# Router on groups of four tiles, and expert counts scanned on VectorE ahead of the rank matmuls

## The chip, the cores and the metric

The kernel runs on one NeuronCore of a Trainium2 chip. The metric is device time in microseconds, the median of three runs. The engines are called PE (TensorE, matmuls), PEld (its weight loads), DVE (VectorE), ACT (ScalarE), POOL (GpSimd) and SP (SyncE, which here only issues DMAs). "q" behind an engine's name is its instruction queue.

## The reference

32 sequences of 64 rows of 512 numbers are first mixed by a 64x64 matrix that is looked up per sequence, then go through a router and a mixture of eight experts (each token takes its two best, an expert takes at most 640), and the result is added to the input.

```python
def cond(x, conditions, weights):
    w = weights[conditions]
    return jnp.einsum('bct,bcd->bdt', x, w)

def ffn(x, Wr, Wg, Wu, Wd):
    N = Bb * Tt
    cap = max(1, int(1.25 * (N * 2 / E)))
    xf = x.reshape(N, Hh)
    logits = jnp.einsum('nh,eh->ne', xf, Wr)
    gate = jax.nn.softmax(logits, axis=-1)
    top2_val, top2_idx = jax.lax.top_k(gate, 2)
    flat_idx = jnp.concatenate([top2_idx[:, 0], top2_idx[:, 1]])
    onehot = jax.nn.one_hot(flat_idx, E, dtype=jnp.int32)
    rank = (jnp.cumsum(onehot, axis=0) * onehot).sum(-1)
    keep = rank <= cap
    ...
    g = jax.nn.silu(jnp.einsum('nh,eih->eni', xf, Wg))
    u = jnp.einsum('nh,eih->eni', xf, Wu)
    out_e = jnp.einsum('eni,ehi->enh', g * u, Wd)
    y = jnp.einsum('ne,enh->nh', comb, out_e)

x = x + ffn(cond(x, itok_B_1_198, cond_weights), Wr, Wg, Wu, Wd)
```

## The kernel before

The 2048 tokens lie in 16 tiles of 128 rows, in pairs m = 0 to 7 (tile j belongs to pair j // 2). The program has two parts. The front finds out which token goes to which expert and writes the conditioned tokens to the DRAM buffer `xf_dram`. The expert part gathers rows of `xf_dram` expert by expert and runs the three projections in split fp32r. All engines have hand-written instruction streams with semaphores; what stands in the source is the order in which each engine works, and an engine stops at each wait.

The front has two strands that meet at the first gather.

The **routing strand**. `x_tile_turn(j)` transposes a tile of x on PE (L1178, four 128x128 transposes into one PSUM bank), ACT (L601) or DVE (L811, tiles 1, 2, 5, 6 and 9) copies it to `turned_sb`. `router(m)` multiplies one pair by the router weights: four matmuls of 256 columns, one for each quarter of the 512 features, each in its own group of 32 PE columns (L1190). DVE copies the result (`xrT_copy`, L818), PE turns it back (`turn`, L1201), DVE adds the four quarters (`xr_sum`, L824), and `logits(g)` multiplies by the conditioning matrices (L1223), in four groups of tiles given by `LG` (6, 4, 4 and 2 tiles). `top_two` finds the two best experts of each token (MAX and MAX_INDEX, one of each for each tile, L832 and L835), and `one_hot` (L845) writes them as ones into `ohp` for tiles 0 to 7 and 8 to 15. After the second one_hot PE sums the counts of each tile over all 128 rows (L1269) and within the tile (L1272); DVE scans the totals (L902), adds the rank within the tile (L905), multiplies by the one-hot (L906) and reduces to one rank for each assignment (L907). From this come slot numbers, the comparison tables `pick_t` and `pick_p` (L924, L927, L930), 32 small PE matmuls that invert the list (L1283) and `src_row` (L951), which releases `lists_ok`.

The **conditioning strand**. `condition(j)` multiplies one pair of x tiles by its matrices on PE (eight matmul records of 512 columns, L1234) into two of four PSUM banks; it waits until ACT has copied the pair before the previous one out of its banks. ACT copies each tile to `xf_sb` (L593), SP stores each pair to `xf_dram` (L390, the last two tiles apart on L394). `condition(0)` to `condition(6)` stand ahead of the rank matmuls on PE, `condition(8)` to `condition(14)` behind them. ACT also makes the rounded high parts of the first expert's weights, `w_high(u)` (L609), one of four between these copies (`W0_EARLY = 1`), three behind them, and DVE the low parts, `w0_low(u)` (L942).

POOL waits for `lists_ok` and for every store (`xf_out`) before its first gather (L508). PE fills the time until that has landed with matmuls whose result is not used (`KEEP_WARM = 18`, L1289), then turns the gathered rows (L1303) and starts the first expert.

SP loads x in eight DMAs of two tiles, then two small ones, places eight tiles' conditioning matrices (L361), loads the first expert's gate and up weights (L372), stores `xf_dram`, then the gates (L396, waits for `gates_ok`), and then loads the first expert's down weights (L376, L379).

## Time and profile before

| | us |
|---|---|
| median of three runs | 274.7 (273.92 to 275.18) |
| the profiled execution | 272.44 |
| its span, first to last instruction | 270.6 |
| PE busy | 257.8 (95% of the span) |
| first gather issued by POOL | 37.55 |
| first gathered rows turned by PE | 42.09 |

The span is read by stretches: up to 42 us the front, then eight experts in which PE is the engine with the most work. An instruction's start and duration in the timeline are read as they stand; what ended the idle time ahead of it stands in brackets behind it.

### The profile page before, as it was taken

To read this page: it belongs to the slowest core of one execution; us is meant where nothing else is said; L and a number is where in the kernel's file an instruction comes from. 1 tells how busy PE (TensorE), PEld (TensorE's weight loads), DVE (VectorE), ACT (ScalarE), POOL (GpSimd) and SP (SyncE) were. 2 spreads that over 40 slices of the span, in tenths; PEclk is the share of its full clock that TensorE was granted. 3 is DMA by queue.
4 is the path that set the end of the run, shared out by engine and by line. 5 is a ranking of instruction groups with operands and counts; after the bars stand their busy time and mean duration, and the time that the engine had idled before them with its cause. 6 is when DMAs were issued, how large, how long until landed. Compare 5 with 4: busy or idle time off the path is not lost.

```text
span 270.6 us, 4016 instructions
## 1 busy us (share of the span) xinstructions
PE 257.8 (95%) x1368; PEld 200.0 (74%) x1368; DVE 161.6 (60%) x332; ACT 137.7 (51%) x242; POOL 173.6 (64%) x156
## 2 busy tenths in 40 slices
PE   8999698999999999999999999999999999999991
PEld 4663156999987867888878887777787777878980
DVE  2658998444459664876566639674865867343251
ACT  2356843444464656565366644664565559442100
POOL 5792048741158867884887478858887886685742
PEclk9999979999999999999999999999999999999998
DMA  6996888999869998899679867998899699366441
GB/s 201 363 300 241 344 270 272 386 338 330 294 193 209 202 207 256 162 216 277 170 130 250 238 178 111 200 294 251 154 238 329 148 192 225 40 79 81 131 177 46
DMA packets 27099, 59.00 MB, mean 218 GB/s; under 512 B 6198, under 2 KB 6454, under 8 KB 26976
## 3 DMA queue, kind: packets, MB, share of 16 engines
q1 hardware_dynamic: 16416, 37.89, 44.3%
q0 software_dynamic: 10656, 20.75, 37.2%
q8 instruction: 16, 0.26, 0.4%
q14 instruction: 11, 0.09, 0.1%
HBM read 39.56 MB, written 20.25 MB: 221 GB/s over the span
## 4 chain that ended last, share of the span: by engine, by line
PE 52%; DVE 3%; ACT 2%; DMA 2%; issue 2%; POOLq 0%; ACTq 0%; DVEq 0%
PE bank L1342 19%; PE bank L1429 17%; PE bank L1437 9%; PE bank L1316 3%; DMA xg<-xf_dram,src_turn 2%; PE bank L1444 2%; PE bank L1452 2%; DVE w L1005 1%; ACT hhi L696 1%; POOLq L85 0%; DVE squares L1054 0%; PE bank L1303 0%; DVE hlo L1060 0%; DVE h L1120 0%; DVE h_last L1100 0%
## 5 line engine op out<-in xcount | busy, mean ns | idle before, releaser
L1429 PE MATMUL bank<-xhi,w 128*128 128x512 f32 x280 | 71.6, 398 | 0.0
L1342 PE MATMUL bank<-w,hhi 128*128 128x512 f32 (+1 forms) x216 | 67.1, 393 | 1.5 <-ACT y_sb L667 1.0
L554 POOL DMA_INDIRECT out<-y_sb,dst_row x35 | 56.5, 1613 | 13.4 <-issue 13.4
L1429 PEld LDWEIGHTS bank<-xhi,w 128*128 128x128 f32 x280 | 52.3, 188 | 13.2 <-DVE h_last L1100 0.8
L520 POOL DMA_INDIRECT gate_g<-gates_dram,src_row x40 | 46.8, 1170 | 12.1 <-issue 11.5
L1342 PEld LDWEIGHTS bank<-w,hhi 128*128 128x128 f32 x216 | 39.2, 188 | 10.7 <-DVE hlo L1060 1.6
L1005 DVE TENSOR_TENSOR w<-raw,w 128x704 fp32r<-128x704 f32 (+1 forms) x35 | 37.1, 1060 | 14.6 <-ACT w L609 8.2
L508 POOL DMA_INDIRECT xg<-xf_dram,src_turn x24 | 25.6, 1065 | 26.0 <-DVE xlo L990 11.6
L1342 PE MATMUL bank<-w,hlo 128*128 128x512 f32 (+1 forms) x108 | 41.9, 388 | 0.0
L1437 PE MATMUL bank<-xlo,w 128*128 128x512 f32 x140 | 38.4, 396 | 0.0
L609 ACT ACTIVATE w<-raw 128x704 fp32r<-128x704 f32 (+1 forms) x40 | 36.7, 923 | 0.0
L508 POOL DMA_INDIRECT xg<-xf_dram,src_row x16 | 18.1, 1130 | 27.5 <-DMA xf_dram<-xf_sb 15.9
L1054 DVE STREAM_TRANSPOSE squares<-xg 128x512 f32<-128x512 f32 x24 | 24.0, 1046 | 16.7 <-DMA xg<-xf_dram,src_turn 16.7
L1437 PEld LDWEIGHTS bank<-xlo,w 128*128 128x128 f32 x140 | 26.4, 189 | 6.4
L667 ACT ACTIVATE y_sb<-bank,gate_g 128x512 f32<-128x512 f32 x30 | 20.1, 686 | 20.0 <-PE bank L1342 18.6
L1342 PEld LDWEIGHTS bank<-w,hlo 128*128 128x128 f32 x108 | 20.3, 188 | 4.6
L1316 PE MATMUL bank<-w,xhi 128*128 128x352 f32 x112 | 20.5, 327 | 0.8 <-ACT xhi L644 0.8
L1316 PEld LDWEIGHTS bank<-w,xhi 128*128 128x128 f32 x112 | 18.2, 189 | 1.4 <-issue 1.0
L696 ACT ACTIVATE hhi<-h 128x512 fp32r<-128x512 f32 x14 | 8.9, 634 | 19.6 <-DVE h L1107 12.0
L1060 DVE TENSOR_TENSOR hlo<-h,hhi 128x512 fp32r<-128x512 f32 x14 | 9.7, 693 | 10.4 <-ACT hhi L696 10.4
L990 DVE TENSOR_TENSOR xlo<-xg,xhi 128x512 fp32r<-128x512 f32 x24 | 15.0, 684 | 1.5 <-ACT xhi L654 1.5
L654 ACT ACTIVATE xhi<-xg 128x512 fp32r<-128x512 f32 x24 | 13.3, 620 | 2.7 <-DMA xg<-squares 2.7
(138 smaller groups left out, 304.8 us busy)
## 6 DMA issues: line engine op xcount, KB each, us to landing
raw<-wgu SPq DMA_DIRECT2D x32, 352.0 KB, 7.8
xg<-squares SPq DMA_DIRECT2D x24, 256.0 KB, 7.5
x_sb<-x SPq DMA_DIRECT2D x8, 512.0 KB, 7.6
raw<-wd SPq DMA_DIRECT2D x8, 512.0 KB
xf_dram<-xf_sb SPq DMA_DIRECT2D x7, 512.0 KB, 3.0
raw<-wd SPq DMA_DIRECT2D x8, 192.0 KB
out<-x SPq DMA_DIRECT2D x1, 1280.0 KB, 18.3
gate_g<-gates_dram,src_row POOLq DMA_INDIRECT x40, 6.5
```

Source lines behind the costliest of these rows:

```text
L508: nc.gpsimd.indirect_dma_start(out=xg[:, t, :], out_offset=None, in_=xf_dram[:, :], in_offset=bass.IndirectOffsetOnAxis(ap=rows, axis=0), ...
L520: nc.gpsimd.indirect_dma_start(out=gate_g[:, n % TPE, :], out_offset=None, in_=gates_dram[:, :], in_offset=bass.IndirectOffsetOnAxis(ap=sr ...
L554: nc.gpsimd.indirect_dma_start(out=out[:, :], in_=y_sb[:, n % TPE, :], in_offset=None, out_offset=bass.IndirectOffsetOnAxis(ap=dst_row[:, ...
L609: last = nc.scalar.activation(w[:, half, 0, a:b], raw[:, a:b], ACT.Copy)
L667: nc.scalar.activation(y_sb[:, t, :], y_bank(e, t)[:, :], ACT.Copy, scale=gate_g[:, t, e:e + 1]).then_inc(y_ok, n)
L990: nc.vector.tensor_tensor(xlo4[:, :, cols], turned_rows(e, t), xhi4[:, :, cols].bitcast(F32), ALU.subtract).then_inc(xlo_ok, n)
L1005: last = nc.vector.tensor_tensor(w[:, half, 1, a:b], raw[:, a:b], w[:, half, 0, a:b].bitcast(F32), ALU.subtract)
L1054: nc.vector.transpose(squares[:, :, t, :], xg[:, t, :].rearrange("p (i b) -> p b i", i=SQ)).then_inc(squares_ok, 1)
L1316: last = nc.tensor.matmul(ps[:, 0:I], left[:, b, c], w[:, half, part, o:o + I], start=(k == 0 and left is xhi and part == 0), stop=(k == K ...
L1342: last = nc.tensor.matmul(ps[:, cols], left(c), w[:, half, part, o:o + width], start=(c == 0 and q == 0), stop=(closes and c == cs[-1] and ...
L1429: last = nc.tensor.matmul(ACC_BANK[what][:, :], columns(what, k, part), xhi4[:, k, :], start=(k == 0 and part == 0), stop=False)
L1437: last = nc.tensor.matmul(ACC_BANK[what][:, :], columns(what, k, 0), xlo4[:, k, :], start=False, stop=(k == KH - 1))
```

## The change

- The router takes four tiles at a time: four matmuls of 512 columns instead of two sets of four with 256. Tiles 0 to 11 keep their turned copy in a buffer of their own (`turned_x`, over memory that is used only later), so the copies no longer wait for the router. `turn`, `xrT_copy` and `xr_sum` also take four tiles; two of the four `xrT` copies are on ACT.
- The last two tiles come from DRAM already turned (a new input `xt`, 512 KB, prepared with the other inputs), and PE doesn't turn them. Their router step is in two halves of 256 columns for each quarter. The natural-order tiles 14 and 15 (`load_x(7)`) are loaded behind the placed matrices.
- `LG` is four groups of four tiles. `top_two` of the last two groups is one block of DVE instructions.
- `condition(0)`, `(2)` and `(4)` stand ahead of the rank matmuls, `condition(6)` to `(14)` behind them; before, `(6)` was ahead too.
- The counts are scanned over tiles and experts on DVE first (`before`, a bf16 tile), and PE multiplies the scan by ones and adds it in PSUM onto the ranks within the tile. DVE then needs one multiply and one reduce.
- Softmax: one subtract for tiles 0 to 11 and one for 12 to 15, one exponential of all tiles on ACT behind its fourteenth `xf_copy`, the sums behind `pick_p`, the gate product behind the lists.
- All four `w_high` of the first expert are behind the sixteen `xf_copy`, all four `w0_low` behind the lists. The first expert waits for two of them ahead of its first half and for four ahead of the second.
- `KEEP_WARM` is 27 instead of 18.

```diff
-LG = ((0, 3), (3, 5), (5, 7), (7, NM))
+LG = ((0, 2), (2, 4), (4, 6), (6, NM))
+RING = 3 * XR
+TURNED = TT - 2
-KEEP_WARM = 18
+KEEP_WARM = 27
...
-            for m in range(2, NM):
+            for m in range(2, NM - 1):
                 load_x(m)
+            sp.dma_start(turned_x[:, RING:RING + 2, :, :],
+                         xt.rearrange("p (r k c) -> p r k c", r=2, k=KH)).then_inc(xt_in, 16)
...
             for j in range(HALF, TT):
                 place(j)
+            load_x(NM - 1)
...
-            sp.wait_ge(gates_ok, 2)
+            sp.wait_ge(gates_ok, 1)
...
+            for g in range(XRT_DVE, NG):
+                act.wait_ge(xrT_ps, g + 1)
+                nc.scalar.activation(xrT[:, g % 2, :], ps_xrT[g][:, :],
+                                     ACT.Copy).then_inc(xrT_ok, 1)
...
+            for n in range(TT):
+                xf_copy(n, n % XR)
+                if n == TT - 3:
+                    act.wait_ge(sub_ok, 2)
+                    nc.scalar.activation(ex[:, :, :], lg[:, :, :], ACT.Exp).then_inc(ex_ok, 1)
+            for u in range(KH):
                 w_high(u, 0, 0)
...
             dve.wait_ge(oh_ok, 2)
+            dve.wait_ge(oh_clear, 1)
+            dve.wait_ge(consts, CONSTS)
+            nc.vector.tensor_tensor_scan(before[:, :, :].rearrange("p e a -> p (e a)"),
+                                         carry[:, :, :].rearrange("p e a -> p (e a)"),
+                                         ohp[:, :, :].rearrange("p e a -> p (e a)"), 0.0,
+                                         ALU.mult, ALU.add).then_inc(before_ok, 1)
+            subtract(0, LG[3][0] * 2)
             dve.wait_ge(rank_ps, 1)
...
-            link(nc.vector.tensor_tensor(rk[:, :, :], run[:, :, 0:A], within, ALU.add))
-            link(nc.vector.tensor_tensor(rk[:, :, :], rk[:, :, :], oh, ALU.mult))
+            ranks = ps_rank.rearrange("p (e a) -> p e a", e=E)
+            nc.vector.tensor_tensor(rk[:, :, :], ranks[:, :, 0:A], oh,
+                                    ALU.mult).then_inc(before_ok, 1)
...
-            for u in range(W0_EARLY):
-                w0_low(u)
...
+            gate_sums()
             dve.wait_ge(slot_ps, 1)
...
+            gates()
+            for u in range(KH):
                 w0_low(u)
...
+            turn_tiles(0, 8)
+            pe.wait_ge(wr_in, 16)
+            router(0)
+            turn_tiles(8, 12)
+            router(1)
+            turn(0)
+            turn_tiles(12, TURNED)
+            turn(1)
+            logits(0)
+            router(2)
+            logits(1)
+            router(3)
             condition(0)
-            router(NM - 1)
-            turn(NM - 2)
-            condition(2)
-            turn(NM - 1)
+            turn(2)
+            turn(3)
             logits(2)
             logits(3)
+            condition(2)
+            condition(4)
...
-            nc.tensor.matmul(ps_total, ones[:, :], o, start=True, stop=True)
...
+                nc.tensor.matmul(ranks[:, :, o_j:A:2], left[:, :], oh[:, :, o_j::2],
+                                 start=(o_j == 0), stop=False)
+            pe.wait_ge(before_ok, 1)
+            for cols in (slice(0, A), slice(A, A + 1)):
+                last = nc.tensor.matmul(ranks[:, :, cols], ones[:, :], before[:, :, cols],
+                                        start=False, stop=(cols.start == A))
             last.then_inc(rank_ps, 1)
-            for j in range(after, TT, 2):
+            for j in range(6, TT, 2):
                 condition(j)
...
                 if s == 0:
-                    pe.wait_ge(wlo0_ok, KH)
+                    pe.wait_ge(wlo0_ok, 2)
...
+                if s == 0:
+                    pe.wait_ge(wlo0_ok, KH)
```

PE's queue around the ranks, before (L1234 is a pair of `condition`, L1269 and L1272 are the rank matmuls, L1283 the list matmuls):

```order
L1234 MATMUL bank<-x_sb,wq 64x512 [waits xf_ok]
L1234 MATMUL bank<-x_sb,wq 64x512 x3
L1269 MATMUL bank_7<-ohp,ones 128x264 [waits oh_clear,oh_ok,consts]
L1272 MATMUL bank_7<-ohp,upper 128x128
L1272 MATMUL bank_7<-ohp,upper_odd 128x128
L1234 MATMUL bank<-x_sb,wq 64x512 [waits xf_ok]
L1234 MATMUL bank<-x_sb,wq 64x512 x3
```

And in the changed program, from the second to the fourth pair (`condition` is L1235, the rank matmuls are L1274 and L1278):

```order
L1235 MATMUL bank<-x_sb,wq 64x512 [waits x_in1]
L1235 MATMUL bank<-x_sb,wq 64x512 x3
L1235 MATMUL bank<-x_sb,wq 64x512 [waits xf_ok,x_in2]
L1235 MATMUL bank<-x_sb,wq 64x512 x3
L1274 MATMUL bank_7<-ohp,upper 128x8x16 [waits oh_clear,oh_ok,consts]
L1274 MATMUL bank_7<-ohp,upper_odd 128x8x16
L1278 MATMUL bank_7<-before,ones 128x8x32 [waits before_ok]
L1278 MATMUL bank_7<-before,ones 128x8
L1235 MATMUL bank<-x_sb,wq 64x512 [waits xf_ok,x_in3]
L1235 MATMUL bank<-x_sb,wq 64x512 x3
```

The pair that waits for `x_in3` (tiles 6 and 7) has moved behind the ranks, and a second wait, for `before_ok`, now stands ahead of it and of all later pairs.

ACT's queue from the last copy of a turned tile, before (L593 is `xf_copy`, L620 the exponential, L609 `w_high`; behind the branch a loop of two rounds with four copies each, of which the first is shown):

```order
L593 ACTIVATE xf_sb<-bank 128x512 [waits xf_ps] x2
L620 ACTIVATE ex<-lg 128x80 [waits sub_ok]
L593 ACTIVATE xf_sb<-bank 128x512 [waits xf_ps] x2
L609 ACTIVATE w<-raw 128x704 [waits raw_in0]
L593 ACTIVATE xf_sb<-bank 128x512 [waits xf_ps] x2
L620 ACTIVATE ex<-lg 128x48 [waits sub_ok]
L593 ACTIVATE xf_sb<-bank 128x512 [waits xf_ps] x2
L634 UNCONDITIONAL_BRANCH
L634 ISA
L593 ISA [waits xf_ps]
L593 ACTIVATE xf_sb<-bank 128x512
```

And in the changed program (L618 is the copy of `xrT`, L605 `xf_copy`, L636 the exponential, L625 `w_high`):

```order
L618 ACTIVATE xrT<-bank_7 128x512 [waits xrT_ps]
L618 ACTIVATE xrT<-bank 128x512 [waits xrT_ps]
L605 ACTIVATE xf_sb<-bank 128x512 [waits xf_ps] x14
L636 ACTIVATE ex<-lg 128x128 [waits sub_ok]
L605 ACTIVATE xf_sb<-bank 128x512 [waits xf_ps] x2
L625 ACTIVATE w<-raw 128x704 [waits raw_in0]
```

Nothing but one exponential stands between the copies now; the weights' high parts are all behind them.

## Rows read from the trace of the kernel before

**Rows 1.** The profile's page, its first lines: span, and PE's busy time.

```profile
span 270.6 us, 4016 instructions
PE 257.8 (95%) x1368; PEld 200.0 (74%) x1368; DVE 161.6 (60%) x332; ACT 137.7 (51%) x242; POOL 173.6 (64%) x156
```

**Rows 2.** Timeline, SP and POOL at the front's end: start, duration, engine, line, instruction.

```profile
35.05 0.65 SPq L376 DMA_DIRECT2D raw<-wd  x1
...
37.55 1.73 POOL L508 DMA_INDIRECT xg<-xf_dram,src_row  x1 [15.88 <-DMA xf_dram<-xf_sb]
```

**Rows 3.** Line L486, POOL's wait for the stores (duration ns, first and last start us).

```profile
L486 POOLq EVENT_SEMAPHORE  x1: 17/17/17, 36.8 to 36.8; - x1
```

**Rows 4.** DMA issues: the last store of xf, and the first gather (us to landing).

```profile
xf_dram<-xf_sb SPq DMA_DIRECT2D x1, 256.0 KB, 3.3
xg<-xf_dram,src_row POOLq DMA_INDIRECT x1, 4.4
```

**Rows 5.** Timeline, ACT's copies of the conditioned tiles, and three w_high behind them.

```profile
27.16 1.09 ACT L593 ACTIVATE xf_sb<-bank 128x512 f32<-128x512 f32 x2
29.02 2.06 ACT L593 ACTIVATE xf_sb<-bank 128x512 f32 x4 [0.76 <-PE bank L1234]
31.40 2.06 ACT L593 ACTIVATE xf_sb<-bank 128x512 f32 x4 [0.32 <-PE bank L1234]
33.35 2.16 ACT L609 ACTIVATE w<-raw 128x704 fp32r<-128x704 f32 x3
```

**Rows 6.** Timeline, PE from the ranks to the first expert.

```profile
27.76 1.95 PE L1234 MATMUL bank<-x_sb,wq 64*64 64x512 f32 x16
33.72 2.53 PE L1283 MATMUL bank<-pick_t,turned_sb 128*128 128x40 f16 x32 [1.50 <-DVE turned_sb L930]
36.08 5.75 PE L1289 MATMUL bank<-iota_q 128*128 128x512 f16 x18
42.09 0.63 PE L1303 MATMUL bank<-ident,xg 128*128 128x128 f32 x4 [0.26 <-DMA xg<-xf_dram,src_row]
```

**Rows 7.** Timeline, PE in the router's stretch, and one burst of weight loads.

```profile
10.92 1.09 PE L1178 MATMUL bank<-ident,x_sb 128*128 128x128 f32 x8
13.75 0.64 PE L1190 MATMUL bank<-turned_sb,wr_sb 128*32 128x256 f32 x8
14.32 0.44 PE L1201 MATMUL bank<-ident,xrT 128*128 128x128 f32 x2
14.59 1.04 PE L1178 MATMUL bank<-ident,x_sb 128*128 128x128 f32 x8
20.73 0.41 PE L1223 MATMUL bank<-xr,wq 64*64 64x8 f32 x16
25.36 0.18 PEld L1234 LDWEIGHTS bank<-x_sb,wq 64*64 64x64 f32 x4 [0.25 <-ACT xf_sb L593]
```

**Rows 8.** Timeline, DVE from a top_two to the rank chain and the tables.

```profile
21.21 0.39 DVE L832 MAX8 v<-bank 128x8 f32<-128x8 f32 x4
22.34 0.24 DVE L864 TENSOR_TENSOR lg<-bank,v 128x80 f32<-128x80 f32 x1
26.86 0.38 DVE L845 TENSOR_TENSOR ohp<-iota_e,i 128x128 bf16<-128x128 f32 x1
27.92 0.70 DVE L902 TENSOR_TENSOR_SCAN run<-carry,bank 128x264 f32<-128x264 f32 x1
29.57 0.59 DVE L907 TENSOR_REDUCE r<-rk 128x32 f32<-128x256 f32 x1
32.89 2.49 DVE L930 TENSOR_TENSOR turned_sb<-iota_q,slot_tp 128x1024 f16<-128x1024 f16 x4
36.29 0.20 DVE L951 TENSOR_SCALAR src_row<-bank 128x40 uint32<-128x40 f32 x1
```

**Rows 9.** Stretches of 0.5 us: PE, PEld, DVE, ACT, POOL busy, then PE's granted clock.

```profile
37.50:38.00 0.50, 0.50 (x3) 0.20 (x2) 0.50 (x2) 0.00 (x0) 0.45 (x1) 0.50 0.93 328
40.50:41.00 0.50, 0.50 (x4) 0.20 (x2) 0.47 (x2) 0.00 (x0) 0.32 (x1) 1.00 0.71 283
```

More of the change, by code:

```diff
@@ L127, in build @@
         oh = ohp[:, :, 1:A + 1]
-        run = sb("run", [P, E, A + 1])
+        before = sb("before", [P, E, A + 1], BF16)
         more = sb("more", [1, E], U16)
@@ L204, in build @@
         wsel_in = sem("wsel_in")
-        row_in = [sem(f"row_in{g}") for g in range(len(LG) - 1)]
-        placed = [sem(f"placed{g}") for g in range(1, len(LG))]
+        row_in = [sem(f"row_in{g}") for g in range(2)]
+        placed = [sem(f"placed{g}") for g in range(2, NG)]
+        xt_in = sem("xt_in")
         tT_ps = sem("tT_ps")
@@ L279, in build, with turned_slot @@
         TURN_DVE = [1, 2, 5, 6, 9]
-        TURN_ACT = [j for j in range(TT) if j not in TURN_DVE]
+        TURN_ACT = [j for j in range(TURNED) if j not in TURN_DVE]
+        def turned_slot(j):
+            return j % RING if j < TURNED else RING + j - TURNED
         def group_of(j):
@@ L849, in one_hot @@
                     ALU.is_equal).then_inc(oh_ok, 1)
[L851 to L860 removed]
+            for j in TURN_DVE[0:4]:
+                turn_copy(j)
+            xrT_copy(0)
+            for j in TURN_DVE[4:]:
+                turn_copy(j)
+            xrT_copy(1)
+            xr_sum(0)
+            xr_sum(1)
+            top_two(0)
+            top_two(1)
+            xr_sum(2)
             def subtract(a, b):
@@ L933, in _ @@
                     ALU.is_equal).then_inc(pick_ok, 1)
-            nc.vector.tensor_scalar(more[:, :].unsqueeze(2), run[0:1, :, A:A + 1],
-                                    -float((TPE - 1) * P), 0.0,
-                                    ALU.add, ALU.max).then_inc(more_ok, 1)
             def w0_low(u):
@@ L967, in _ @@
                                     ALU.add).then_inc(lists_ok, 1)
-            for u in range(W0_EARLY, KH):
+            gates()
+            for u in range(KH):
                 w0_low(u)
@@ L1180, in x_tile_turn, with router @@
                 last.then_inc(tT_ps, 1)
-            def router(m):
-                for j in (m * 2, m * 2 + 1):
+            def router(g):
+                for j in range(g * XR, min((g + 1) * XR, TURNED)):
                     turned(j)
-                if m >= 1:
-                    pe.wait_ge(xrT_ok, m)
-                r = m * 2 % XR
+                if g == NG - 1:
+                    pe.wait_ge(xt_in, 16)
+                if 1 <= g < NG - 1:
+                    pe.wait_ge(xrT_ok, g)
@@ L1203, in turn @@
+                last.then_inc(xrT_ps, 1)
+            def turn(g):
+                pe.wait_ge(xrT_ok, g + 1)
+                if 1 <= g < NG - 1:
+                    pe.wait_ge(xr_ok, g)
+                for j in range(XR):
+                    last = nc.tensor.transpose(ps_xr[g][:, j * P:(j + 1) * P],
+                                               xrT[:, g % 2, j * P:(j + 1) * P], ident[:, :])
                 last.then_inc(xr_ps, 1)
@@ L1216, in logits @@
                 if by_place:
-                    pe.wait_ge(placed[g - 1], 16 * len(by_place))
+                    pe.wait_ge(placed[g - 2], 16 * len(by_place))
                 if 0 < g < 3:
```

173 lines of the change are left out of this document (62 added, 111 removed).

## The prediction

> **What bounds the kernel now.** I read three views in this order. The page gives the span and PE's share: 95% of 270.6 us [rows 1]. From 42 us on PE has little idle time, so a change of the front is worth what it moves the moment at which PE turns the first gathered rows, 42.09 us [rows 6], nearly one for one. The timeline's end of the front then tells what sets that moment. Two strands meet at the first gather. The lists: `src_row` is written at 36.29 and done at 36.49 [rows 8]. The stores of xf: ACT's last copy ends at 31.40 + 2.06 = 33.46 [rows 5], the last store lands 3.3 us behind its issue [rows 4], and POOL's wait ends at 36.8 [rows 3]. So the stores come last, by 0.3 us; the two strands are nearly level. The gather starts at 37.55 [rows 2] and lands 4.4 us later [rows 4], PE turns at 42.09. From the end of the last copy to that turn it is 42.09 - 33.46 = 8.63 us.
>
> The third view is ACT's and PE's rows of the conditioning strand. Copies run in groups of four tiles of 2.06 us with gaps of 0.76 and 0.32 us that PE ends [rows 5]. Four tiles and a gap are 2.38 us: two PSUM pairs turn over between an engine that needs 0.98 us for a pair (1.95 for two [rows 6]) and one that needs 1.03. What sets the last copy is therefore the moment at which PE resumes conditioning behind the ranks, 27.76 us [rows 6], and how many pairs are left then: four.
>
> **The router's stretch, step by step.** x arrives as before up to tile 7; PE turned tiles 6 and 7 at 10.92 [rows 7] as they landed, and that stays, since the DMAs ahead of them are the same. What changes is that the gaps ahead of it held routers before and stay empty now. So I start the new PE sequence at 10.92 and add it up:
> - turning tiles 6 to 13, four pairs: a pair occupies PE for 0.98 us until the router's start at the pace of [rows 7]; 3.9;
> - four routers: four matmuls of 512 columns in four column groups are not in the trace. A set of 256 columns holds PE 0.57 us (13.75 to 14.32 [rows 7]); four matmuls of 512 columns in four quadrants hold it 0.98 us [rows 6]. The bounds are 0.57 and 1.14 (two sets); I take 0.98, the row with the same number of columns; 3.9;
> - four turns of four tiles: two take 0.27 until the next instruction (14.32 to 14.59 [rows 7]); 0.5 each; 2.0;
> - logits of four tiles 0.3 to 0.4 each (0.41 for sixteen records [rows 7]); 1.3; `condition(0)` 0.98;
> - new waits: `logits(1)` waits for the first `top_two`, 1.13 us long for four tiles (21.21 to 22.34 [rows 8]), which `router(2)` covers but for 0.4; `logits(2)` and `(3)` wait for two reduces, 0.7.
>
> Together 13.2 us: `logits(3)` ends near 24.1. Then `top_two` of eight tiles: one of four takes 1.13, the MAX part of the first four overlaps the last logits, so 1.9 to its end; subtract and one_hot 0.5. The second one_hot ends at about T = 26.45, against 26.86 + 0.38 = 27.24 [rows 8]. The routing strand gains 0.8 us up to here. `condition(2)` and `(4)` lie in PE's wait, and cost nothing as long as they end by T: 24.1 + 2 x 0.98 = 26.1, just so.
>
> **The ranks.** Before, PE's rank matmuls needed only the one_hot, and `condition(8)` stood 0.52 us behind T (27.76 - 27.24). Now the DVE scan stands between: 0.70 us [rows 8] and a semaphore to each side. PE can resume at T + 0.05 + 0.70 + 0.3 = T + 1.05 = 27.5; the 0.3 for the semaphore and the ones matmul is an estimate from the 0.52, which held the same steps and three matmuls. What is queued behind that wait on PE is all remaining conditioning, five pairs now. For DVE the chain is shorter: before, the reduce (L907) ended at 29.57 + 0.59 = T + 2.92 [rows 8], after two gate steps and the add; now scan, the ones matmul, multiply and reduce give T + 2.35. The tables follow as before (5.2 us to the end of `pick_p`, 35.38, [rows 8]): `pick_p` ends at 26.45 + 2.35 + 5.2 = 34.0.
>
> **The conditioning strand, which decides.** The first pair behind the ranks leaves PE 0.98 later, and ACT starts its copy at 27.5 + 1.26 = 28.8 (before, 27.76 to 29.02 [rows 5, 6]). Five pairs are two groups of four tiles and one pair: 28.8 + 2.06 + 0.32 + 2.06 + 0.32 + 1.03 = 34.6. The one exponential fits into the second gap (its wait for the subtracts is long over). Removing `w_high` (0.8 us) between the early copies gives nothing: these copies now end long before PE resumes. So the last copy ends at 34.6 instead of 33.46: **+1.1 us**. The moment of resuming gained 0.26 us, the fifth pair costs 1.35.
>
> **Behind it.** PE ends conditioning near 33.4, when three of four `pick_p` are written, and needs about 2.4 us for the 32 list matmuls (2.53 [rows 6]): 35.8. The lists are then ready at 36.1, some 0.4 earlier than before, which buys nothing, since the stores land at 36.8 + 1.1 = 37.9. The gather starts at 38.65 and lands at 43.1. The warm matmuls: 18 took 5.75 us [rows 6], with the granted clock at 0.50 (1.2 GHz) in a part of it and 1.00 (2.4 GHz) again by 40.5 [rows 9]. About 3.4 us at the lower clock and 2.35 at the higher make 0.225 us for one at full clock, and nine more 2.0 us. From 35.8 they end at 35.8 + 5.75 + 2.0 = 43.6, half a us behind the landing, and the turn waits for that: 43.7. If the clock doesn't fall they end at 41.9 and the landing sets 43.2. So the turn is 1.1 to 1.6 us later. A third piece pulls the same way: the gates' product stands behind the lists now, so SP stores the gates and loads the first down weights (704 KB, issued at 35.05 before [rows 2]) some 3 us later, right into the gather's transfer; zero to 0.5 us, and partly under the warm matmuls' overrun. I take +1.5 for the sum.
>
> What has cover: the four `w_high` (2.16 for three [rows 5]) end at 37.5 and the four `w0_low` near 41, before PE's first use near 44.4. The copies of `src_turn` stand behind them and are the thinnest cover: they end about when ACT has the first rounded rows, and would cost if the lists came later. The 512 KB of `xt` are in the place of x's last pair; that pair, behind the placed matrices, is needed only at 32 us. The relaxed wait for the first expert's weights releases nothing that is late.
>
> **Sum.** 272.44 + 1.5 = 273.9 in a profiled execution like the one shown, whose span is 270.6; on the median of the three runs 274.7 + 1.5 = **276.2 us**. The measurement can tell about 0.5%, 1.4 us, from no change; the forecast lies on that edge.
>
> **Rivals.**
> (1) *The last router is slow.* It puts two matmuls on one column group and then goes on to the next. If the next group can't start before the second half has, it holds PE for 3 x 0.49 + 0.98 = 2.45 us instead of 0.98. T, PE's resuming and all that follows are 1.5 us later: 277.7. Against it: in two successive pairs of `condition`, the weights of four quadrants are loaded in one burst at 25.36 [rows 7], while earlier passes still ran in each, so a waiting quadrant didn't hold up the others. A depth of more than two waiting passes isn't in the trace, so half of the price is possible too. The Trainium skill, TensorE: Matmul & The Clock Gate, Part 3 (The mechanism), says that matmuls start and end strictly in program order and only weight loads are pulled ahead; by that rule this rival is the outcome. The same price would arise if PE's granted clock fell from 1.00 to 0.50 in the stretches that are empty now, ahead of 10.92 and around 27 us. Chance 0.2.
> (2) *The front is level or gains.* If a router of 512 columns cost 0.6 us like one of 256, T would be 25.0 and PE would resume at 26.1; the last copy ends at 33.2, and the stores at 36.5. The point from which this decides is a resuming at 26.4 us or earlier. Then the turn is at 41.8 and the time 274.4; and if ACT's gaps of 0.76 and 0.32 are its loop's branches, which the change unrolls, rather than PE's lag, up to 1.0 more goes: 273.4. For it: the row of 256 is not at its columns' rate alone. Against it: the condition rows, which are. Chance 0.2 with gains of under 1.4 us, and 0.1 for more (the clock of the warm stretch would have to help).
> (3) *The change doesn't reach the end.* The expert part absorbs a late start (its gathers and the DVE chain in the middle have slack of their own): then about 274.9. PE is busy 95% [rows 1], so it can absorb little. Chance 0.1.
>
> **Numbers.** Forecast case, +0.9 to +2.1 us (275.6 to 276.8): 0.4, the likeliest, and three fifths of it lie above 1.4 us. Slower by over 0.5%: 0.24 + 0.2 = 0.44. Within 0.5%: 0.16 of the forecast, 0.2 of rival (2), 0.1 of rival (3), 0.46. Faster: 0.1. The range takes in rival (1) at its full price, 277.7, and rival (2) nearly down to its 273.4: 273.6 to 277.8.
>
> **What would show it.** In the new profile: ACT's last `xf_copy` ends near 34.6, POOL's wait ends near 37.9 and the first gathered rows are turned near 43.6. The scan starts at 26.5 and the pair of tiles 6 and 7 at 27.5. The last router's row is near 1.0 us (2.4 in rival 1). If the last copy ends by 33.5, my step on the routers is wrong; if it ends at 34.6 but the time doesn't move, the step from the front to the end is.

## The result and the profile after

| | before | after |
|---|---|---|
| median of 20 runs each, us | 273.39 (271.68 to 363.4) | 276.56 (273.99 to 282.41) |
| ratio, 95% interval | | 1.0089 (1.0060 to 1.0118) |
| the profiled execution, us | 272.44 | 277.79 |
| its span, us | 270.6 | 276.0 |

The change makes the kernel slower by 0.9%, about 2.4 us by the ratio. (Disturbed executions are left out of the ratios, which is why ratio and medians differ a little.) The profiled execution of after is one of the longer ones. Its timeline is read first at the front's end, as for the kernel before.

The page's first lines (as [rows 1]):

```profile
span 276.0 us, 3924 instructions
PE 259.8 (94%) x1346; PEld 202.9 (74%) x1346; DVE 158.7 (57%) x317; ACT 137.8 (50%) x241; POOL 176.0 (64%) x156
```

Timeline of PE from the last router to conditioning's resumption (as [rows 6, 7]; start, duration, engine, line):

```profile
19.79 1.09 PE L1189 MATMUL bank<-turned_x,wr_sb 128*32 128x256 f32 x16
20.81 1.09 PE L1235 MATMUL bank<-x_sb,wq 64*64 64x512 f32 x8
...
26.98 0.30 PE L1278 MATMUL bank<-before,ones 128*128 128x256 bf16 x2
27.21 1.52 PE L1235 MATMUL bank<-x_sb,wq 64*64 64x512 f32 x12
```

The last router (L1189), with two halves on each column group, holds PE for 20.81 - 19.79 = 1.02 us. Conditioning resumes at 27.21.

Timeline of DVE (as [rows 8]) and of ACT (as [rows 5]):

```profile
25.80 0.38 DVE L842 TENSOR_TENSOR ohp<-iota_e,i 128x128 bf16<-128x128 f32 x1
26.21 0.71 DVE L890 TENSOR_TENSOR_SCAN before<-carry,ohp 128x264 bf16<-128x264 bf16 x1
...
35.70 0.20 DVE L940 TENSOR_SCALAR src_row<-bank 128x40 uint32<-128x40 f32 x1 [1.62 <-PE bank L1289]
```

```profile
28.37 2.06 ACT L605 ACTIVATE xf_sb<-bank 128x512 f32<-128x512 f32 x4 [1.39 <-PE bank L1235]
30.75 2.07 ACT L605 ACTIVATE xf_sb<-bank 128x512 f32<-128x512 f32 x4 [0.31 <-PE bank L1235]
32.70 0.31 ACT L636 ACTIVATE ex<-lg 128x128 f32<-128x128 f32 x1
33.12 1.10 ACT L605 ACTIVATE xf_sb<-bank 128x512 f32<-128x512 f32 x2
```

The second one_hot ends at 26.18, `src_row` is written at 35.70 (36.29 before), and the last copy ends at 34.22 (33.46 before). So the lists came 0.6 us earlier and the copies 0.8 us later, as foreseen.

SP's two last stores, each from a window of its own; POOL's wait for all stores (duration ns, start us), and its first gather (as [rows 2, 3]):

```profile
33.75 1.21 SPq L406 DMA_DIRECT2D xf_dram<-xf_sb  x1
35.01 0.69 SPq L406 DMA_DIRECT2D xf_dram<-xf_sb  x1
L498 POOLq EVENT_SEMAPHORE  x1: 17/17/17, 39.2 to 39.2; - x1
39.93 1.39 POOL L520 DMA_INDIRECT xg<-xf_dram,src_row  x1 [18.35 <-DMA xf_dram<-xf_sb]
```

And the DMA view at the last store's issue, us to landing (as [rows 4]):

```profile
xf_dram<-xf_sb SPq DMA_DIRECT2D x1, 256.0 KB, 4.2
```

Here is the first part of the surprise. The wait ends 5.0 us behind the last copy (39.2 - 34.22), where it was 3.3 before (36.8 - 33.46).

PE from the lists on (as [rows 6]), and its granted clock (the last but two of the columns; as [rows 9]):

```profile
33.00 2.59 PE L1289 MATMUL bank<-pick_t,turned_sb 128*128 128x40 f16 x32
35.41 6.01 PE L1295 MATMUL bank<-iota_q 128*128 128x512 f16 x27
43.97 0.72 PE L1309 MATMUL bank<-ident,xg 128*128 128x128 f32 x4 [2.55 <-DMA xg<-xf_dram,src_row]
45.46 2.68 PE L1322 MATMUL bank<-w,xhi 128*128 128x352 f32 x8 [0.78 <-ACT xhi L643]
...
54.74 0.60 PE L1309 MATMUL bank<-ident,xg 128*128 128x128 f32 x4
```

```profile
43.00:44.00 1.00, 0.03 (x1) 0.06 (x2) 0.44 (x3) 0.00 (x0) 0.82 (x1) 1.00 0.69 152
44.00:46.00 2.00, 1.22 (x6) 0.93 (x7) 0.65 (x1) 1.28 (x2) 1.57 (x2) 0.60 0.75 176
46.00:48.00 2.00, 2.00 (x9) 2.00 (x8) 1.32 (x2) 0.69 (x1) 1.80 (x3) 0.50 0.98 359
48.00:50.00 2.00, 2.00 (x10) 1.93 (x9) 0.48 (x1) 0.00 (x0) 1.70 (x2) 0.50 1.01 396
```

Here is the second part of the surprise. The first turn is 1.9 us later (43.97 against 42.09), but the turn of the third gathered tile is 4.6 us later (54.74 against 50.11). The 27 kept-warm matmuls ran at full clock and ended at 41.42. PE then stood idle for 2.55 us, and the granted clock was 0.50 (1.2 GHz) in the first expert, until 51 us. Before, the low clock lay in the kept-warm stretch, where it costs nothing. From the first to the third turn it takes 10.77 us, before 8.02: 2.75 us for the clock.

### The profile page after: what moved, and what is told of

Same layout as the page of the kernel before. It is cut to its first block, busy times and chain, and to the rows that moved or that the text cites. A ratio compares the mean times of both kernels' runs of the same rounds, so it can differ in the third digit from the quotient of the medians.

```text
span 276.0 us, 3924 instructions
## 1 busy us (share of the span) xinstructions
PE 259.8 (94%) x1346; PEld 202.9 (74%) x1346; DVE 158.7 (57%) x317; ACT 137.8 (50%) x241; POOL 176.0 (64%) x156
## 4 chain that ended last, share of the span: by engine, by line
PE 68%; DMA 11%; DVE 6%; issue 5%; ACT 5%; POOL 3%; SPq 1%; POOLq 1%; ACTq 0%; DVEq 0%
PE bank L1348 23%; PE bank L1437 15%; PE bank L1322 11%; PE bank L1445 7%; DMA out<-y_sb,dst_row 3%; DMA x_sb<-x 3%; PE bank L1309 2%; ACT xf_sb L605 2%; PE bank L1235 2%; DVE w L995 2%; DMA xg<-xf_dram,src_turn 2%; DVE squares L1044 2%; POOL gate_g L532 2%; DMA xf_dram<-xf_sb 2%; PE bank L1167 1%
## 5 line engine op out<-in xcount | busy, mean ns | idle before, releaser
L532 POOL DMA_INDIRECT gate_g<-gates_dram,src_row x40 | 50.2, 1255 | 12.1 <-issue 11.2
L1348 PE MATMUL bank<-w,hlo 128*128 128x512 f32 (+1 forms) x108 | 41.9, 388 | 0.0
L520 POOL DMA_INDIRECT xg<-xf_dram,src_row x16 | 17.2, 1073 | 32.7 <-DMA xf_dram<-xf_sb 18.3
L625 ACT ACTIVATE w<-raw 128x704 fp32r<-128x704 f32 (+1 forms) x40 | 36.5, 922 | 0.0
L1044 DVE STREAM_TRANSPOSE squares<-xg 128x512 f32<-128x512 f32 x24 | 24.6, 1055 | 17.7 <-DMA xg<-xf_dram,src_turn 17.6
L1322 PE MATMUL bank<-w,xhi 128*128 128x352 f32 x112 | 22.3, 348 | 0.8 <-ACT xhi L643 0.8
L1322 PEld LDWEIGHTS bank<-w,xhi 128*128 128x128 f32 x112 | 19.9, 205 | 1.5 <-issue 1.1
```

Source lines behind the costliest of these rows:

```text
L520: nc.gpsimd.indirect_dma_start(out=xg[:, t, :], out_offset=None, in_=xf_dram[:, :], in_offset=bass.IndirectOffsetOnAxis(ap=rows, axis=0), ...
L532: nc.gpsimd.indirect_dma_start(out=gate_g[:, n % TPE, :], out_offset=None, in_=gates_dram[:, :], in_offset=bass.IndirectOffsetOnAxis(ap=sr ...
L625: last = nc.scalar.activation(w[:, half, 0, a:b], raw[:, a:b], ACT.Copy)
L1044: nc.vector.transpose(squares[:, :, t, :], xg[:, t, :].rearrange("p (i b) -> p b i", i=SQ)).then_inc(squares_ok, 1)
L1322: last = nc.tensor.matmul(ps[:, 0:I], left[:, b, c], w[:, half, part, o:o + I], start=(k == 0 and left is xhi and part == 0), stop=(k == K ...
L1348: last = nc.tensor.matmul(ps[:, cols], left(c), w[:, half, part, o:o + width], start=(c == 0 and q == 0), stop=(closes and c == cs[-1] and ...
```

## Experiments

Every run was timed beside the kernel before on the same chip, but e1 to e4, e5 to e8 and e9 to e12 each had a chip of their own. So it is the ratios that can be compared from run to run, not the medians. All front times are of one profiled execution each, in us. "Fetch" is the start (cut off to a tenth) of the fetch of PE's instructions that lies nearest to the stores' end: one packet of 16 KB on the DMA queue that the profile calls q8, instruction. That it is PE's is read from e7, e9 and e12, where edits of PE's stream alone moved it. "To third" is the time from the first to the third turn.

| kernel | last copy ends | stores' wait ends | fetch | first turn | to third | median (runs) | ratio, 95% interval |
|---|---|---|---|---|---|---|---|
| before | 33.46 | 36.8 | 36.8 | 42.09 | 8.02 | 273.39 (20) | |
| after | 34.22 | 39.2 | 33.0 | 43.97 | 10.77 | 276.56 (20) | 1.0089 (1.0060 to 1.0118) |
| e1, six ahead | 33.87 | 38.3 | 32.7 | 42.86 | 8.06 | 276.32 (6) | 1.0113 (1.0055 to 1.0172) |
| e2, warm 38 | 34.36 | 39.0 | 33.1 | 44.09 | 8.03 | 275.24 (12) | 1.0037 (1.0007 to 1.0067) |
| e3, before, five behind | 34.67 | 38.6 | 37.9 | 43.39 | 8.06 | 275.89 (12) | 1.0031 (0.9988 to 1.0074) |
| e4, six ahead, warm 36 | 33.08 | 38.0 | 31.9 | 42.85 | 8.05 | 274.76 (12) | 1.0047 (1.0020 to 1.0074) |
| e5, before, scan first | 34.55 | 37.9 | none | 42.52 | 10.57 | 276.32 (6) | 1.0111 (1.0055 to 1.0167) |
| e6, one store | 34.57 | 39.0 | 33.4 | 43.38 | 8.03 | 276.01 (6) | 1.0128 (1.0064 to 1.0192) |
| e7, 40 small matmuls | 34.04 | 39.1 | 36.4 | 43.74 | 10.79 | 277.24 (6) | 1.0155 (1.0100 to 1.0210) |
| e8, six, 40 small, warm 33 | 32.87 | 37.5 | 36.2 | 42.63 | 8.06 | 274.76 (12) | 1.0070 (1.0036 to 1.0104) |
| e9, 28 small matmuls | 34.37 | 37.7 | 37.3 | 43.47 | 9.43 | 276.39 (6) | 1.0144 (1.0087 to 1.0202) |
| e10, eight ahead, warm 29 | 33.46 | 38.2 | 32.3 | 43.84 | 8.00 | 275.20 (12) | 1.0064 (1.0027 to 1.0101) |
| e11, eight, 28 small, warm 29 | 34.80 | 38.1 | 38.5 | 45.90 | 8.02 | 275.40 (8) | 1.0092 (1.0058 to 1.0126) |
| e12, e5 with warm 29 | 34.52 | 40.0 | 37.8 | 44.28 | 8.06 | 275.79 (6) | 1.0122 (1.0080 to 1.0163) |

The first turn of e10 is set by its kept-warm matmuls, not by the gather. In e11's profile the granted clock is 0.50 from 12 to 14 us already and the second one_hot ends 1.5 us later than in e10 (27.77 against 26.23), so of its front only the stretch from the last copy to the wait's end is used.

Single profiles differ in more than the edit: the second one_hot ends at 26.38 in e1 and at 25.56 in e4, whose programs are the same up to there. What lies behind the third turn isn't constant either. The span less the third turn is 220.5 us in before, 221.3 in after, and from 220.6 (e6) to 223.5 (e7, e10) in the others. In e3, e7 and e10 the clock falls to 0.50 once more, for about 3 us from 101 or 105 us on. So a difference of 1 us at the first turn can't be expected to show in a ratio of six to twelve executions.

**Which pair stands behind the ranks (e1, e4, e3).** The step that the prediction rests on. e1 puts `condition(6)` ahead of the ranks again, e4 does this with 36 kept-warm matmuls; e3 is the kernel before with one pair (two tiles) fewer ahead.

```diff
             condition(4)
+            condition(6)
...
-            for j in range(6, TT, 2):
+            for j in range(8, TT, 2):
```

```diff
-BEFORE_RANKS = 4
+BEFORE_RANKS = 2
```

> The changed kernel with the pair of tiles 6 and 7 conditioned ahead of the rank matmuls again, as in the kernel before. Theory A (the stores of xf decide, and the fifth pair behind the ranks is what made them late): the last copy ends at 33.1 instead of 34.2 us, POOL's wait for the stores ends near 37.8 instead of 39.2, the first gathered rows are turned near 42.6 instead of 44.0, and the time falls by 1.2 to 2 us against the changed kernel. Rival B (the lists or the gather itself decide): POOL's wait ends as before the edit and the time stays. Rival C (what costs is PE's low clock in the first expert, whatever the moment of the turn): the turn comes earlier, the time doesn't follow.

> The changed kernel with the pair of tiles 6 and 7 ahead of the ranks and 36 warm matmuls. If A and C both hold, the turn is near 42.6 us with PE working up to it and the first expert at full clock: about level with the kernel before (ratio 0.998 to 1.003). If only A holds, it equals the run with the pair alone.

> The kernel before with one edit: the pair of tiles 6 and 7 stands behind the rank matmuls (two early pairs and one more instead of two). Theory A: the last copy ends 1.2 us later, 34.65 us, the stores land 1.2 us or more later, the turn follows, and the time rises by 1.2 to 2 us (ratio 1.004 to 1.008). Rival B (slack elsewhere takes it up): the time stays within 0.5 us. The rank chain isn't touched, so the lists stay at 36.5 us in both.

In e3 the last copy moved by 1.2 us (33.46 to 34.67) for one more pair behind; in e1 and e4 it came 0.35 and 1.1 us earlier than in after. Measured from the end of the second one_hot, which takes out when x arrived, the last copy ends 7.5 us behind it in e1 and e4 and 8.0 in after; it is 6.2 in before and 7.5 in e3. So one pair more behind the ranks costs 1.3 us in the kernel before and 0.5 us in the changed one, where `condition(6)` ahead of the ranks itself holds up PE's resuming (28.08 in e1, 1.7 us behind the one_hot instead of 1.03). But e4 showed that this isn't all: its last copy ends 0.4 us earlier than in the kernel before, and the stores' wait still ends 1.2 us later.

What the pair is worth in time none of these runs shows. e1's first turn is 1.1 us earlier than that of after, and its ratio (1.0113) is no lower. e4's is 1.2 us earlier than that of e2, at full clock in both profiles, and the ratios are 1.0047 and 1.0037. e3's interval takes in both no change and the 0.4 to 0.8% that was expected.

**The kept-warm stretch (e2).** Only the count is changed, 38 for 27.

```diff
-KEEP_WARM = 27
+KEEP_WARM = 38
```

> The changed kernel with 38 warm matmuls instead of 27, eleven more at 0.22 us each: they end at 41.4 + 2.4 = 43.8 us, just ahead of the landing at 44.0 (if the granted clock stays at 1.00 in them). Theory C (PE's idle time of 2.55 us ahead of the turn lets the clock fall to 0.50 in the first expert, which costs 2.8 us there): the first expert runs at 1.00, and the time falls by 2 to 3 us against the changed kernel, although the turn isn't earlier. Rival: the clock falls anyway, in the warm stretch (then little is lost or won) or in the expert (then the time stays or grows by the overrun).

Timeline of PE in this kernel:

```profile
35.55 8.38 PE L1295 MATMUL bank<-iota_q 128*128 128x512 f16 x38
44.09 0.63 PE L1309 MATMUL bank<-ident,xg 128*128 128x128 f32 x4 [0.16 <-DMA xg<-xf_dram,src_row]
45.49 1.50 PE L1322 MATMUL bank<-w,xhi 128*128 128x352 f32 x8 [0.78 <-ACT xhi L643]
```

The first turn comes 0.1 us later than in after, the idle 2.55 us are filled, and the first gate and up group takes 1.50 us instead of 2.68. The third turn is at 52.12 against 54.74. The ratio falls from 1.0089 to 1.0037, by 1.4 us; the two intervals overlap a little, so this may be anything from a few tenths to 2.6 us. The estimate is less than the 2.6 us of the profile. The low clock doesn't come in every execution of after: the mean granted clock of its 20 lies between 0.970 and 0.998, the longest times at the lowest clocks; in e2 ten of twelve have 0.993 or more, in after four of 20. The profiles of e1 and e6, with 27 matmuls as well, show none of it ahead of the third turn (8.06 and 8.03 us).

**Why the stores land late (e6, e7, e9).** Three theories: SP issues the last stores late; five pairs in one row are late by themselves; or a fetch of PE's instructions, which in after falls into the middle of the stores, holds one of the 16 DMA engines. The DMA view of after, in the half us from 33.0, and the stretch where nearly all engines are done (the last two columns are DMA share and GB/s; one of 16 engines is 0.06):

```profile
q8 instruction: 1, 0.02, 18.7%
```

```profile
37.00:37.50 0.50, 0.50 (x4) 0.23 (x3) 0.50 (x2) 0.50 (x1) 0.00 (x0) 1.00 0.07 29
37.50:38.00 0.50, 0.50 (x4) 0.19 (x2) 0.50 (x2) 0.50 (x1) 0.00 (x0) 1.00 0.06 25
```

18.7% of 16 engines in 0.5 us is 1.5 us on one engine, and from 37.0 to 38.0 one engine alone still moves packets of the stores. e6 stores the last pair in one DMA:

```diff
-            for m in range(NM - 1):
+            for m in range(NM):
...
-            for j in range(TT - 2, TT):
-                sp.wait_ge(xf_ok, j + 1)
-                sp.dma_start(xf_t[:, j:j + 1, :], xf_sb[:, j:j + 1, :]).then_inc(xf_out, 16)
```

e7 and e9 put matmuls of one column into PE's idle time ahead of tiles 4 and 6, 14 and 26 of them in e7, 10 and 18 in e9, and do nothing else:

```diff
-            turn_tiles(0, 8)
+            turn_tiles(0, 4)
+            for _ in range(10):
+                nc.tensor.matmul(bank[4][0:1, 0:1], warm[:, 0:1], warm[:, 0:1], start=True, stop=True)
+            turn_tiles(4, 6)
+            for _ in range(18):
+                nc.tensor.matmul(bank[4][0:1, 0:1], warm[:, 0:1], warm[:, 0:1], start=True, stop=True)
+            turn_tiles(6, 8)
```

> The changed kernel, with the last pair of conditioned tiles stored by one DMA behind the sixteenth copy instead of two behind the fifteenth and sixteenth. In the changed kernel SP's issues of the two last stores take 1.21 and 0.69 us, and POOL's wait ends at 39.2, 5.0 us behind the last copy (34.22). Theory P (issue): the stores land late because SP issues them late, one behind the other. Then one store fewer is issued at 34.3 and lands some 0.5 to 0.7 us earlier; POOL's wait ends at 38.5 to 38.7, the first turn comes 0.6 us earlier, the ratio to the kernel before is about 0.002 below that of the changed kernel. Theory Q (one of the 16 DMA engines is late with its share of earlier stores, behind PE's instruction fetch at 33.0 us in the middle of the stores): POOL's wait ends at 39.2 as in the changed kernel and nothing moves; the DMA share again stands at 0.06 or 0.07, one engine of sixteen, ahead of the wait's end.

> The changed kernel, with 40 matmuls of one column (results unused, into a PSUM bank that is free then) in PE's idle time while it waits for x, 14 ahead of tiles 4 and 5 and 26 ahead of tiles 6 and 7. They do no work and should fit into the 0.42 and 1.21 us in which PE is idle there. They push PE's later instructions further back in its stream, so each fetch of PE's instructions (16 KB on one DMA queue; one at 33.0 us, in the middle of the stores) comes earlier by 40 instructions and more, ahead of the stores' burst that starts at 30.3. Theory Q (the fetch makes one DMA engine late with its share of the stores): POOL's wait ends near 37.9 instead of 39.2, the gather is issued near 38.7, the first turn comes near 42.9 instead of 43.97, and the time goes down by about 1 us (ratio to the changed kernel about 0.996). Theory R (the burst of five pairs fills the DMA engines and the lateness is its own): the fetch moves, POOL's wait still ends at 39.0 to 39.3 and the time stays. Theory P (issue): the same as R.

> The changed kernel with 28 instead of 40 small unused matmuls in PE's idle time ahead of tiles 4 to 7 (10 and 18). With 40 of them the fetches of PE's instructions came at 25.6 and 36.4 us, so one fell into the end of the stores again, as the one at 33.0 did in the changed kernel; in the kernel before with the scan first, where none fell between 26 and 50 us, the last store landed 3.3 us behind its issue. With 28 the fetches should come near 28 and near 41. Theory Q (a fetch among the stores makes one DMA engine late): no fetch lies between the stores' start at 29.4 and their end, the last store lands 3.3 us behind its issue instead of 4.2, POOL's wait ends at 37.4 to 37.8 instead of 39.2, and the first turn comes at 42.1 to 42.5. Theory R (five pairs stored without a pause are late by themselves): the fetch is out of the way and POOL's wait still ends at 38.8 or later. If the fetch lands elsewhere than foreseen the run says nothing on this.

With one store (e6) the wait ends at 39.0, with the issue no longer held up. But e6's last copy ends 0.35 us later than in after, and from there to the wait's end it is 4.45 us instead of 4.95. So SP's issue was worth about 0.5 us, and 1.1 us of the delay stayed without it: it was at most a part of the cause. In e7 the fetches moved to 25.6 and 36.4, so that another one fell among the last stores, and nothing was gained; taken alone, e7 would have spoken for the second theory. In e9 they lie at 25.9 and 37.3. Its POOL wait and gather, the last store's row at its issue, and the DMA engines in the second of the two stretches shown for after:

```profile
L498 POOLq EVENT_SEMAPHORE  x1: 17/17/17, 37.7 to 37.7; - x1
38.46 1.38 POOL L520 DMA_INDIRECT xg<-xf_dram,src_row  x1 [16.72 <-DMA xf_dram<-xf_sb]
xf_dram<-xf_sb SPq DMA_DIRECT2D x1, 256.0 KB, 3.3
37.50:38.00 0.50, 0.50 (x4) 0.24 (x3) 0.50 (x1) 0.50 (x1) 0.00 (x0) 1.00 0.00 0
```

The wait ends 1.5 us earlier than in after, though the last copy ended 0.15 later: five pairs stored in a row land 3.3 us behind the last issue, as four do, when the fetch comes only as their last parts land. In after 0.9 of the 1.5 us are in the last store's landing (4.2 against 3.3), and 0.6 in SP's issue of it, which stood behind one that took 1.21 us.

The other profiles agree. Each store lands in 16 parts, whose moments the trace has. In before, e5 and e11, where no fetch starts before the last part has landed, the last 16 parts land within 0.3 us. In after all but three had landed by 37.38, and those came at 37.93, 38.55 and 39.17. In e1 to e4, e6 to e8, e10 and e12 one to three parts come up to 0.7 to 2.2 us behind the rest, in e9 one comes 0.2 behind. That speaks for the fetch, and against five pairs in a row. How one packet of 1.0 to 1.5 us holds a part up by more than its own time isn't shown.

What clearing the fetch did not bring is time: the first turn came only 0.5 us earlier, and the ratio (1.0144) is no lower than that of after (1.0089). The gather took 5.0 us from issue to turn instead of 4.0; the down weights (SP, issued at 37.74 and 38.79) were on the DMA engines with it, at a DMA share of 1.0 from 40.0 to 41.5. That it was they that held up the gather is argued, not shown; and PE's clock fell again behind 1.90 us of idle time.

**The scan ahead of the rank matmuls, alone (e5), and with a filled idle stretch (e12).** e5 is the kernel before with the scan and the matmul with ones of after.

```diff
+            nc.vector.tensor_tensor_scan(before[:, :, :].rearrange("p e a -> p (e a)"),
+                                         carry[:, :, :].rearrange("p e a -> p (e a)"),
+                                         ohp[:, :, :].rearrange("p e a -> p (e a)"), 0.0,
+                                         ALU.mult, ALU.add).then_inc(before_ok, 1)
             dve.wait_ge(rank_ps, 1)
...
+            pe.wait_ge(before_ok, 1)
+            for cols in (slice(0, A), slice(A, A + 1)):
+                last = nc.tensor.matmul(ranks[:, :, cols], ones[:, :], before[:, :, cols],
+                                        start=False, stop=(cols.start == A))
             last.then_inc(rank_ps, 1)
```

```diff
-KEEP_WARM = 18
+KEEP_WARM = 29
```

> The kernel before, with one part of the change: the counts are scanned on DVE first and PE adds the scan by a matmul with ones in PSUM onto the ranks, so all later conditioning pairs on PE stand behind a wait for DVE's scan. Nothing else moves. Before, PE resumed conditioning 0.52 us behind the end of the second one_hot (27.76 against 27.24). My step in the prediction: it resumes 1.05 us behind it, at 28.3; four pairs are left, so ACT's last copy ends at about 34.0 instead of 33.46, POOL's wait for the stores ends at 37.3 instead of 36.8, and the first turn is at 42.6 instead of 42.09: +0.5 us, a ratio of about 1.002. DVE's chain to the end of the reduce is 2.35 us from the one_hot's end instead of 2.92, which buys nothing while the stores come last. Rival: the wait for the scan is hidden (PE resumes at 27.8 as before) and the shorter chain gives 0.1 to 0.5 us back, ratio 0.998 to 1.000.

> The kernel before with the scan first, and 29 instead of 18 kept-warm matmuls. With 18 the first turn came at 42.52 (0.43 us later than before), yet the time was 3 us longer: PE stood idle for 2.55 us ahead of that turn, its granted clock was 0.50 from 42 to 48 us, and the third turn of the first expert came 3.0 us later than before. Theory K (the clock, not the later turn, is what most of those 3 us are): with 29 matmuls the warm stretch ends at 42.3, the turn stays at 42.5, the first expert runs at clock 1.00, and the ratio falls from 1.011 to 1.001 to 1.003. Rival: the clock falls elsewhere or the time is lost further on, and the ratio stays at 1.008 or more.

DVE and PE of e5 around the ranks, and PE at the front's end:

```profile
26.82 0.38 DVE L846 TENSOR_TENSOR ohp<-iota_e,i 128x128 bf16<-128x128 f32 x1
27.27 0.20 DVE L875 TENSOR_REDUCE sm<-ex 128x6 f32<-128x48 f32 x1
27.51 0.19 DVE L876 RECIPROCAL sm<-sm 128x6 f32<-128x6 f32 x1
27.73 0.21 DVE L877 TENSOR_TENSOR gate<-ex,sm 128x48 f32<-128x48 f32 x1
27.86 0.70 DVE L898 TENSOR_TENSOR_SCAN before<-carry,ohp 128x264 bf16<-128x264 bf16 x1
28.85 1.52 PE L1234 MATMUL bank<-x_sb,wq 64*64 64x512 f32 x12
35.91 4.06 PE L1291 MATMUL bank<-iota_q 128*128 128x512 f16 x18
42.52 1.09 PE L1305 MATMUL bank<-ident,xg 128*128 128x128 f32 x4 [2.55 <-DMA xg<-xf_dram,src_row]
```

PE resumed 1.65 us behind the one_hot, not 1.05: three gate steps, 0.6 us, stand ahead of the scan in DVE's queue here, and they had cost nothing as long as PE didn't wait for DVE. The last copy moved by 1.1 us. The first turn moved by only 0.4, yet the ratio of 1.0111 is 3.0 us, and the profile shows where: 10.57 us to the third turn, at the low clock, behind 2.55 us of idle time. PE was idle for only 0.25 us ahead of the list matmuls (1.50 in before), and the kept-warm stretch ran at full clock and ended at 39.97. That the one is the reason for the other is argued, not shown.

e12 was to tell the clock from the later turn, and failed at it: 11 more matmuls moved the fetch from beyond 50 us to 37.8, the last store then took 5.4 us instead of 3.3, and the turn came at 44.28. It did take the low clock away (8.06 us to the third turn), but the turn is 1.8 us later and the ratio stayed (1.0122 against 1.0111), as the rival had it. So what the clock is worth in e5's 3.0 us rests on the profile and on e2, not on this run.

**A version that might beat both (e8, e10, e11).** In e4 the lists are ready 3 us ahead of the stores (`src_row` is written at 34.63, the wait ends at 38.0), so still more conditioning could go ahead of the ranks. The edits are those of e1 (e8) or the same with `condition(8)` ahead too (e10, e11), the small matmuls of e7 (e8) and e9 (e11), and the counts of kept-warm matmuls in the table.

> The changed kernel with condition(6) ahead of the ranks again, the 40 small matmuls of the run on the fetch, and 33 instead of 27 matmuls of the kept-warm stretch. With condition(6) ahead the last copy ended at 33.08, yet the wait for the stores ended at 38.0. Theory Q: with the fetch out of the burst POOL's wait ends 3.6 to 3.8 us behind the last copy, at 36.8, the gather is issued at 37.5, the first turn comes at 42.0, with PE's clock at 1.00 from the lists to the first expert (33 x 0.225 = 7.4 us from about 34.7): the time is that of the kernel before, ratio 0.998 to 1.001. Theory R: the wait ends at 38.0 again and the turn is at 42.8, ratio 1.003 to 1.005.

> The changed kernel with condition(6) and condition(8) ahead of the ranks and 29 matmuls of the kept-warm stretch. With six ahead the lists were ready 2 to 3 us before the stores, so another pair moved ahead should cost nothing at the lists' end: src_row 1.2 us later (35.6 against 34.4), still ahead of the stores. ACT's copies then follow one another without a wait for the ranks: last copy at 32.5 to 32.7 instead of 33.1. Theory A (the last copy sets the gather, with what lies behind it): POOL's wait ends 0.4 us earlier than with six ahead, at 37.6 if a fetch falls among the stores and at 36.0 if not; the turn is at 42.2 or 41.2; ratio 1.000 to 1.004. Rival: the list strand takes over (src_row behind 36.5) and the turn is at 42.5 or later, ratio above 1.004.

> The run with condition(6) and condition(8) ahead and 29 kept-warm matmuls, with the 28 small unused matmuls as well, to bring PE's instruction fetch ahead of the stores. It is the version that should come closest to the kernel before or beat it. Theory Q: last copy at 32.6, last store lands 3.3 us behind its issue, POOL's wait ends at 36.0 to 36.4, the gather is issued at 36.8 to 37.1 (37.55 in the kernel before), the first turn comes at 41.2 to 41.6 (42.09 before): ratio 0.996 to 1.000. Theory R: no difference from the same kernel without the small matmuls; the wait ends at 37.4 or later, ratio 1.000 to 1.004.

None beats the kernel before. e8 brings the wait's end to 37.5 and the turn to 42.63, the closest of the changed kernel's versions, at a ratio of 1.0070. In e10 the lists came later (`src_row` 36.16), PE stood idle for 1.2 us ahead of the list matmuls, the low clock fell into the kept-warm stretch and stretched it to 8.12 us: the turn waited for it, at 43.84. The rival stated there, the lists, takes over at eight. e11, which was expected at 0.996 to 1.000, came to 1.0092, no better than e10. In its profile the fetch lies behind the stores and the wait ends 3.3 us behind the last copy, as foreseen, so here too a fetch moved away brought no time. By the intervals, e2, e3, e4, e8 and e10 can't be told from each other.

## Why the prediction was right, point by point

The forecast was 276.2 us, the median is 276.56, within the range. Its mechanism for the front, one more pair behind the ranks and a last copy and a first turn that come later, is what the profiles show; that the time follows the turn nearly one for one, no run shows. That the number came so near is in part luck. The base was 274.7 and is 273.39 over more runs, so the change of +1.5 that I forecast stands against +2.4 (1.6 to 3.2): a base 1.3 us too high made up for a change 0.9 us too small. The +2.4 lies outside the forecast case's +0.9 to +2.1, and the outcome is the slower one, to which I gave 0.44, against 0.46 for no difference.

- *Router and top_two.* Right: T = 26.18 against my 26.45. Rival (1) is out: 1.02 us for the last router. By the rule of strict program order I had named beside it (the Trainium skill, TensorE: Matmul & The Clock Gate, Part 3, The mechanism) it would have been 2.45; eight passes, two on each of four column groups, went through like four of 512 columns.
- *Resuming at T + 1.05.* 27.21 - 26.18 = 1.03. Right in after; e5 shows that it hung on what else stands in DVE's queue.
- *The last copy.* 34.22 against 34.6. Right, and 0.8 us later than before, with the resuming 0.55 us earlier: the fifth pair cost 1.3, as in the forecast (1.35) and in e3.
- *From the last copy to the wait's end.* Wrong, and this is a term I took over without a look: 3.3 us became 5.0. I read SP's queue but not the instruction fetches, which are a row of the DMA view. The page counts 92 instructions fewer, PE's are in another order, and a fetch that lay at 36.8 us now lies at 33.0. Worth 1.5 us at the gather by e9.
- *The kept-warm stretch and the turn.* I had 43.6 with a clock that falls in it and 43.2 with one that doesn't; it was 43.97. The case without a fall I counted as the better one. It was the worse one. Idle time came between the stretch's end (41.42; I had 41.9) and the landing, and behind it the low clock fell into the first expert instead of into matmuls that do nothing: 2.75 us in that execution, about 1.4 in the ratio by e2. This term was missing from the sum.
- *Gates and down weights, 0 to 0.5 us.* PE turned the first rows 4.0 us behind the gather's issue, sooner than before (4.5). e9 has 5.0, so the upper bound is perhaps too low once the stores are earlier.
- *Rivals (2) and (3).* The front's gain reached the lists (0.6 us) but not the stores. What was lost did reach the end in the profile: the third turn is 4.6 us later and the span 5.4 us longer. For a single microsecond at the first turn the runs don't show it (e1 and e4 above).

From e2's ratio and e9's first turn the two missing terms are 1.4 and up to 0.5 us. With them the sum would be 1.5 + 1.9 = 3.4, just above the interval of the measured change (3.2 at most); the sum is no closer than that. What e9 and e11 leave open is why stores that land earlier don't make the ratio smaller.

## What to carry to other kernels

Where matmuls only fill a wait, count them to the landing by the clock they will really have: better control of an earlier stall can take the low clock out of the filler and put it into the first real work. Look where the fetches of an engine's instructions fall among transfers that something waits for; a change of a few dozen instructions moves them. Before an engine is made to wait for another one's result, read what else is queued ahead of that result.

## What the hardware showed that I had not expected

- One fetch of PE's instructions, a packet of 16 KB, took 1.5 us of one DMA engine in after, while the stores kept all of them busy, 1.0 us among the stores of e1 and e6, and 1.0 us at 37.3 in e9, when they were all but done. A transfer that is spread over all engines is complete only when the slowest is. The last store of 256 KB landed 3.2 to 3.3 us behind its issue in before, e5, e9 and e11, and 3.9 to 5.4 us in the kernels with a fetch among the stores or at their very end (e1, e3, e4, e7, e8, e10, e12 and after); in e2 it took 3.5, but its issue was held up by one of 1.54 us.
- In e12 the fetch took 0.96 us (6.0% of 16 engines in 1.0 us) and the store under it landed 2.1 us late. The fetch began at 37.88, when 15 of the store's 16 parts had landed (by 37.80); the last one came at 39.96. The fetch alone doesn't explain the other 1.1 us; this stays open.
- PE's granted clock stayed at 1.00 from the router to the turn in after, through an idle 0.84 us. It fell to 0.50 at the turn or within 1 us behind it where PE had been idle for 2.55, 2.55, 2.50 and 1.90 us ahead of it (after, e5, e7, e9), and not where that was 1.95, 1.68 and 1.62 us (e12, e1, e6). The idle times with a fall and without one overlap, so their length alone doesn't tell.
